# A second transfer of the edge features replaced by a copy on ScalarE

## The chip, the cores and the metric

The kernel runs on one core of one Trainium2 chip. The metric is the device time of one execution in microseconds; three executions of the kernel before took 4943.95, 4955.2 and 4957.94 us, median 4955.2.

## The reference, cut to what matters

A graph layer on 12,500 nodes with 64 features and 412,500 edges with 32 features each, sorted by destination. Everything is float32.

```
h    = relu(layernorm(x))
h0   = edge_attr @ W0 + b0                       # 32 -> 64, for every edge
g    = gelu(gelu(h0) @ W1 + b1) @ W2 + b2        # 64 -> 64 -> 64
score = (h0 + g) @ W3 + b3                       # 64 -> 64
msg  = h[src] * score
sums = segment_sum(msg, dst);  cnt = number of edges of each dst
out  = x + (sums / max(cnt, 1)) @ Wo + bo
```

## The kernel before, in words

The edges are cut into 403 blocks of 1024, each in two halves of 512. Since everything behind the second gelu is linear, the kernel multiplies W2, W0, b0, b2, b3 with W3 once, into a 97-row matrix `w_last`; its right-hand side is `act_in`, with 64 rows of the second gelu, 32 rows of the raw edge features and one row of ones. So the edge features of a block are needed twice: as `pair` (64 partitions, the two halves one above the other, 512 columns) for the first matmul, and as rows 64 to 95 of `act_in` (32 partitions, the two halves side by side) for the last. Both come from DRAM, in two transfers of 128 KB.

A block passes these steps, each named by its function or line:

- `gather` (L329), GpSimd: eight indirect transfers per block that fetch the normalised rows of `h` for 128 source nodes each, into a ring of 16 blocks. After the first 16 blocks, GpSimd waits before each block b+16 for the message of block b, and before every second one also for the score of block b+8 (`LAG`, L350). This is the only thing that stops it.
- `first` (L431), TensorE: `pair` times W0, to `ps_h0`. Bumps h0_done.
- ScalarE, first gelu (L386), to `g1`. Then the second gelu (L391), in two instructions, from `ps_h1` to `act_in`, once `second` is done.
- `second` (L437), TensorE: `g1` times W1, to `ps_h1`.
- `last` (L446), TensorE: eight tiles of `act_in`, 97 by 128, times `w_last`, to `ps_s`. It waits for the second transfer of the block (`attr_in`, L441) and for both gelus.
- `message` (L615), VectorE: score times gathered rows, to `msg`. It waits for `last` and for the gather.
- `sums` (L455), TensorE: `msg` of eight tiles times a one-hot matrix (L607) of the destinations within a window of 64, to `ps_w`; VectorE adds it to `acc` (L720).

TensorE's order in the steady state is written out by hand (`step`, L502): second(b), first(b+1), sums(b-1), last(b). ScalarE's is first gelu of b, second gelu of b, and so on. The names `ps_sa` and `ps_sb` in the profile are the buffers of even and odd blocks; the same holds for the other pairs.

The SP queue issues the loads. For each block b its loop `ahead` (L277) waits for h0_done of b, issues the `pair` load of block b+4, waits for the score of b, and issues the `act_in` load of block b+4; both buffers are rings of four (`IN_RING`). Once per eight blocks it waits for a message and loads gather indices.

Before the loop come the layernorm of all nodes (VectorE and ScalarE), with the raw rows of the first six blocks gathered meanwhile, and the window plan of the blocks; near the end, after block 390, the output of most nodes is made between two blocks.

Of the kernel before, what the change touches and what calls it, by code (L numbers as in the profile page):

```python
# [24 lines left out]
ACT = mybir.ActivationFunctionType  # L25
AX_X = mybir.AxisListType.X

P = 128
N = 12500
D = 64  # L30
DE = 32
E = 412500
TILES = 8
HALF = TILES // 2 * P
# [16 lines left out]
IDX_GROUPS = 4  # L51
LAG = 8
IN_RING = 4
RAW = 6
LN_ROWS = 25
SPLIT = 112
# [18 lines left out]
def edge_gated_layer(nc, x, edges, src, dst, dst_rows, weights, out):  # L75

    with ExitStack() as ctx:
        def sb(name, shape, dt=F32):
            return ctx.enter_context(nc.sbuf_tensor(name, shape, dt))
# [4 lines left out]
        def sem(name):  # L84
            return ctx.enter_context(nc.semaphore(name))
# [33 lines left out]

        idx = sb("idx", [P, IDX_GROUPS, IDX_GROUP, TILES], I32)  # L120
        pair = sb("pair", [2 * DE, IN_RING, HALF])
        act_in = sb("act_in", [D + DE + 1, IN_RING, 2, HALF])
        g1 = sb("g1", [P, 2, HALF])
        rows = sb("rows", [P, G_RING, TILES, D])

# [4 lines left out]
        fill = sb("fill", [P, 2])  # L130
# [33 lines left out]
        plan_ready = sem("plan_ready")  # L164

        pair_in = [sem(f"pair_in{s}") for s in range(IN_RING)]
        attr_in = [sem(f"attr_in{s}") for s in range(IN_RING)]
        idx_in = [sem(f"idx_in{q}") for q in range(IDX_GROUPS)]
        gathered = [sem(f"gathered{s}") for s in range(G_RING)]
        h0_done = sem("h0_done")  # L170
        g1_done = sem("g1_done")
        h1_done = sem("h1_done")
        g2_done = sem("g2_done")
        score_done = sem("score_done")
        gathers_begun = sem("gathers_begun")
        first_hot = sem("first_hot")
# [20 lines left out]

        jobs = [(LN_ROWS, NP)] * LN_STEPS + [(2 * TILES, P)] * (RAW // 2)
        ln_y = ln_d[0:EP, :, :, :].rearrange("p k n d -> p (k n) d")
# [16 lines left out]
        def uses(b, ring):  # L216

            return (b >> ring.bit_length() - 1) + 1
# [8 lines left out]
        def _(sp):  # L227
# [6 lines left out]
            def load_pair(b, s):  # L234
                sp.dma_start(pair[:, s % IN_RING, :],
                             edges[one(b), :, :, :].rearrange("o g f j -> (o g f) j")
                             ).then_inc(pair_in[s % IN_RING], 16)

            def load_attr(b, s):
                sp.dma_start(act_in[D:D + DE, s % IN_RING, :, :],  # L240
                             edges[one(b), :, :, :].rearrange("o g f j -> f (o g) j")
                             ).then_inc(attr_in[s % IN_RING], 16)

            load_idx(0, 0)
            for c in range(LN_STEPS):
                cols = slice(c * LN_ROWS, (c + 1) * LN_ROWS)
# [8 lines left out]
            sp.dma_start(wp[:, :], weights).then_inc(weights_in, 16)  # L255
            for b in range(2):
                load_pair(b, b)
                load_attr(b, b)
            load_idx(1, 1)
            sp.dma_start(dst_i[:, :, :], dst).then_inc(dst_in, 16)  # L260
            for b in range(2, IN_RING):
                load_pair(b, b)
                load_attr(b, b)
            for part in range(2, IDX_GROUPS):
                load_idx(part, part)
            sp.dma_start(x_late[:, :, :], x[N_EARLY:N, :].rearrange("(t p) d -> p t d", p=NP)
# [9 lines left out]

            def ahead(b, s):  # L277

                sp.wait_ge(h0_done, b + 1)
                load_pair(b + IN_RING, s + IN_RING)  # L280

                sp.wait_ge(score_done, b + 1)
                load_attr(b + IN_RING, s + IN_RING)

            GROUPS = -(-NB // IDX_GROUP)
            TURNS = GROUPS // IDX_GROUPS - 1
# [31 lines left out]
        def _(pool):  # L318
# [14 lines left out]

            for b in range(RAW):
                gather(b, b, x)
# [20 lines left out]
        @block.scalar  # L356
        def _(act):

            def ln_act(k, n, parts):
                act.wait_ge(ln_centred, k + 1)  # L360
                if k >= 2:

                    act.wait_ge(ln_var_ready, k - 1)
                act.activation(ln_sq[0:parts, k % 2, 0:n, :], ln_d[0:parts, k % 4, 0:n, :],
                               ACT.Square).then_inc(ln_squared, 1)

            def ln_root(k, n, parts):
                act.wait_ge(ln_var_ready, k + 1)
                act.activation(ln_std[0:parts, k % 4, 0:n], ln_var[0:parts, k % 4, 0:n],
                               ACT.Sqrt).then_inc(ln_std_ready, 1)  # L370

            def store_h(k):
                act.wait_ge(h_ready, k + 1)
                cols = slice(k * LN_ROWS, (k + 1) * LN_ROWS)
                for p0, p1 in ((0, SPLIT), (SPLIT, NP)):
                    act.dma_start(h_nodes[p0:p1, cols, :], ln_d[p0:p1, k % 4, :, :]).then_inc(h_out, 16)

            def clear_acc(k):
                n = (N + WIN) // LN_STEPS
                act.activation(acc[:, k * n:(k + 1) * n], fill[0:DC, 0:1].to_broadcast([DC, n]), ACT.Copy  # L380
                               ).then_inc(acc_zero, 1)

            def gelus(b, s):

                act.wait_ge(h0_done, b + 1)
                act.activation(g1[:, s % 2, :], ps_h0[s % 2][:, :], ACT.Gelu, bias=b0  # L386
                               ).then_inc(g1_done, 1)

                act.wait_ge(h1_done, b + 1)
                for g in range(2):  # L390
                    act.activation(act_in[0:D, s % IN_RING, g, :],  # L391
                                   ps_h1[s % 2][g * D:(g + 1) * D, :], ACT.Gelu,
                                   bias=wp[g * D:(g + 1) * D, C_B1:C_B1 + 1]
                                   ).then_inc(g2_done, 1)


            act.wait_ge(fill_ready, 1)
            act.activation(act_in[D + DE:D + DE + 1, :, :, :].rearrange("p s g j -> p (s g j)"),
                           fill[D + DE:D + DE + 1, 1:2].to_broadcast([1, IN_RING * 2 * HALF]),
                           ACT.Copy).then_inc(ones_ready, 1)  # L400
            for k in range(LN_STEPS + 1):
                if k < LN_STEPS:
                    ln_act(k, *jobs[k])
                if k >= 1:
                    ln_root(k - 1, *jobs[k - 1])
                if k >= 2:
                    store_h(k - 2)
                if k >= 1:
                    clear_acc(k - 1)
            store_h(LN_STEPS - 1)  # L410
            act.wait_ge(weights_in, 16)
            gelus(0, 0)
            for k in range(LN_STEPS, len(jobs) + 1):
                if k < len(jobs):
                    ln_act(k, *jobs[k])
                if k > LN_STEPS:
                    ln_root(k - 1, *jobs[k - 1])
            blocks_loop(act, 1, NB, IN_RING, gelus)


        @block.tensor
        def _(pe):
# [15 lines left out]
                          ).then_inc(h1_done, 1)  # L438

            def last(b, s):  # L440
                pe.wait_ge(attr_in[s % IN_RING], uses(b, IN_RING) * 16)  # L441

                pe.wait_ge(g2_done, (b + 1) * 2)
                for t in range(TILES):
                    g, j = t % 2, t // 2
                    mm = pe.matmul(ps_s[s % 2][:, t * D:(t + 1) * D],  # L446
                                   act_in[:, s % IN_RING, g, j * P:(j + 1) * P],
                                   w_last[:, :], start=(t == 0), stop=(t == TILES - 1),
                                   skip_group_check=True)
                mm.then_inc(score_done, 1)  # L450
# [340 lines left out]
def one(b):  # L791

    return bass.ds(b, 1)
# [52 lines left out]
```

## Time and profile before

| | |
|---|---|
| median of three runs | 4955.2 us (4943.95 to 4957.94) |
| profiled execution | 4910.35 us, its span 4908.4 us |
| granted TensorE clock | 0.999 of full speed |
| TensorE busy, matmuls | 3760.6 us, 77% of the span |
| TensorE busy, weight loads | 2533.1 us, 52% |
| GpSimd busy | 3082.5 us, 63% |
| ScalarE busy | 987.5 us, 20% |
| VectorE busy | 708.9 us, 14% |
| DMA engines | 46 GB/s; the software queue (gathers) 9.9%, the SP queue 8.4% |

All shares are over the whole span. A busy share says how full an engine is, not what it waits for; idle time of an engine costs only where the engine is the one that others wait for. In the rows below, a timeline row gives the start in us, the duration in us, the engine, the line, the operation, and in brackets how long the engine was idle before and what the profile names as releaser. "remote" as releaser means that the profile found no instruction of this core whose end fits the end of the wait.

### The profile page before, as it was taken

Reading aid. Unit: us, or ns where it says so; the run is one execution under the profiler, and the core shown is the slowest. Engines: PE = TensorE matmul, PEld = TensorE weight load, DVE = VectorE, ACT = ScalarE, POOL = GpSimd, SP = SyncE. Lnnn points to the kernel's source line nnn. Section 1 sums busy time; section 2 is a strip of 40 time slices with the busy share of each in tenths; the row PEclk is TensorE's granted clock in tenths of the full one; section 3 lists DMA queues with packets and bytes.
Section 4 is the critical chain, followed back from the end, with each engine's and each line's share of the span. In section 5 each row is a group of like instructions: output and inputs, shape, how many; then the busy total and the mean of one; then the engine's idle time right before and its main releaser. Section 6 shows DMA issues by size and latency. Waiting matters only on the chain.

```text
span 4908.4 us, 44284 instructions
## 1 busy us (share of the span) xinstructions
PE 3760.6 (77%) x14718; PEld 2533.1 (52%) x14719; DVE 708.9 (14%) x1349; ACT 987.5 (20%) x1332; POOL 3082.5 (63%) x3228
## 2 busy tenths in 40 slices
PE   2487777777777777777777777777777777777788
PEld 1355555555555555555555555555555555555566
DVE  5011111111111111111111111111111111111122
ACT  3112112221122211221122211222112121121211
POOL 7366666666666666666666666666666666666661
PEclk9999999999999999999999999999999999999999
DMA  4111111111111111111111111111111111111111
GB/s 122 28 46 44 45 44 46 46 45 44 44 46 46 44 45 44 46 47 44 44 45 45 46 44 44 44 45 47 44 44 46 44 47 44 44 46 44 46 37 47
DMA packets 223796, 227.46 MB, mean 46 GB/s; under 512 B 118540, under 2 KB 118669, under 8 KB 223352
## 3 DMA queue, kind: packets, MB, share of 16 engines
q0 software_dynamic: 103136, 105.82, 9.9%
q1 hardware_dynamic: 119968, 117.76, 8.4%
q10 hardware_dynamic: 616, 3.20, 0.2%
q14 instruction: 68, 0.56, 0.0%
q8 instruction: 8, 0.13, 0.0%
HBM read 220.11 MB, written 6.40 MB: 46 GB/s over the span
## 4 chain that ended last, share of the span: by engine, by line
another core or an unknown queue 63%; PE 25%; DVE 4%; DVEq 3%; issue 3%; POOL 1%; ACT 0%; DMA 0%; ACTq 0%; POOLq 0%
PE ps_sb L446 14%; PE ps_wa L455 8%; DVE msg L615 3%; DVEq L715 2%; POOL rows L329 1%; DVEq L614 1%; PE ps_sa L446 1%; PE ps_h1a L437 0%; PE ps_h0a L431 0%; PE ps_h0b L431 0%; PE ps_wb L455 0%; PE ps_h1a L484 0%; PE ps_h1b L437 0%; DVE acc L720 0%
## 5 line engine op out<-in xcount | busy, mean ns | idle before, releaser
L329 POOL DMA_INDIRECT rows<-h_rows,idx x3175 | 3026.5, 953 | 1739.0 <-issue 1005.5
L455 PE MATMUL ps_wa<-ln_sq,msg 128*65 128x64 f32 x3230 | 407.2, 319 | 1035.2 <-DVE msg L615 1035.2
L455 PEld LDWEIGHTS ps_wa<-ln_sq,msg 128*65 128x65 f32 x3230 | 369.7, 229 | 1348.6 <-DVE msg L615 1335.1
L391 ACT ACTIVATE act_in<-ps_h1b,wp 64x512 f32<-64x512 f32 x402 | 275.0, 684 | 2446.5 <-remote 2377.6
L446 PE MATMUL ps_sa<-w_last,act_in 97*128 97x64 f32 x3232 | 729.9, 420 | 11.1 <-ACT act_in L391 9.2
L446 PE MATMUL ps_sb<-w_last,act_in 97*128 97x64 f32 x3216 | 728.1, 421 | 0.6 <-ACT act_in L391 0.6
L446 PEld LDWEIGHTS ps_sa<-w_last,act_in 97*128 97x128 f32 x3232 | 711.9, 332 | 13.0 <-ACT act_in L391 9.0
L446 PEld LDWEIGHTS ps_sb<-w_last,act_in 97*128 97x128 f32 x3216 | 710.4, 333 | 2.3 <-issue 1.5
L615 DVE TENSOR_TENSOR msg<-ps_sa,rows 128x512 f32<-128x512 f32 x202 | 139.7, 691 | 3034.6 <-remote 2973.3
L391 ACT ACTIVATE act_in<-ps_h1a,wp 64x512 f32<-64x512 f32 x404 | 276.4, 684 | 1308.7 <-PE ps_h1a L437 1019.2
L455 PEld LDWEIGHTS ps_wb<-ln_sq,msg 128*65 128x65 f32 x3216 | 368.1, 229 | 303.5 <-issue 302.9
L437 PE MATMUL ps_h1b<-g,wp 128*128 128x512 f32 x402 | 406.4, 1112 | 35.7 <-ACT g L386 29.9
L431 PE MATMUL ps_h0a<-pair,wp 64*128 64x512 f32 x404 | 418.5, 1137 | 1.9 <-issue 1.9
L437 PE MATMUL ps_h1a<-g,wp 128*128 128x512 f32 x404 | 408.3, 1114 | 15.1 <-ACT g L386 13.4
L431 PE MATMUL ps_h0b<-pair,wp 64*128 64x512 f32 x402 | 416.5, 1138 | 0.0
L455 PE MATMUL ps_wb<-ln_sq,msg 128*65 128x64 f32 x3216 | 405.6, 319 | 1.5 <-issue 1.5
L615 DVE TENSOR_TENSOR msg<-ps_sb,rows 128x512 f32<-128x512 f32 x201 | 139.0, 692 | 985.9 <-PE ps_sb L446 905.8
L607 DVE TENSOR_TENSOR ln_sq<-dst_i,iota 128x512 f32<-128x512 f32 x403 | 277.8, 690 | 8.4 <-issue 8.4
L431 PEld LDWEIGHTS ps_h0a<-pair,wp 64*128 64x128 f32 x404 | 101.2, 309 | 304.3 <-issue 304.2
L431 PEld LDWEIGHTS ps_h0b<-pair,wp 64*128 64x128 f32 x402 | 100.3, 310 | 302.4 <-issue 302.4
L386 ACT ACTIVATE g<-ps_h0b,wp 128x512 f32<-128x512 f32 x201 | 138.2, 687 | 89.9 <-PE ps_h0b L431 51.5
L386 ACT ACTIVATE g<-ps_h0a,wp 128x512 f32<-128x512 f32 x202 | 138.9, 688 | 12.4 <-PE ps_h0a L431 5.5
(63 smaller groups left out, 719.4 us busy)
## 6 DMA issues: line engine op xcount, KB each, us to landing
pair<-in_edges SPq DMA_DIRECT2D x403, 128.0 KB
act_in<-in_edges SPq DMA_DIRECT2D x403, 128.0 KB
rows<-h_rows,idx POOLq DMA_INDIRECT x3175
xs<-in_x SPq DMA_DIRECT2D x4, 700.0 KB
h_rows<-ln_d ACTq DMA_DIRECT2D x4, 700.0 KB
dst_i<-in_dst SPq DMA_DIRECT2D x1, 1612.0 KB
idx<-in_src SPq DMA_DIRECT2D x50, 32.0 KB
rows<-in_dst_rows SPq DMA_DIRECT2D x4, 384.0 KB
```

The source lines that it names most:

```text
L329: pool.indirect_dma_start(rows[:, slot, t, :], None, table, bass.IndirectOffsetOnAxis(ap=idx[:, part, at, t:t + 1], axis=0),).then_inc(gat ...
L386: act.activation(g1[:, s % 2, :], ps_h0[s % 2][:, :], ACT.Gelu, bias=b0).then_inc(g1_done, 1)
L391: act.activation(act_in[0:D, s % IN_RING, g, :], ps_h1[s % 2][g * D:(g + 1) * D, :], ACT.Gelu, bias=wp[g * D:(g + 1) * D, C_B1:C_B1 + 1]). ...
L431: pe.matmul(ps_h0[s % 2][:, :], w0, pair[:, s % IN_RING, :], start=True, stop=True).then_inc(h0_done, 1)
L437: pe.matmul(ps_h1[s % 2][:, :], w1, g1[:, s % 2, :], start=True, stop=True).then_inc(h1_done, 1)
L446: mm = pe.matmul(ps_s[s % 2][:, t * D:(t + 1) * D], act_in[:, s % IN_RING, g, j * P:(j + 1) * P], w_last[:, :], start=(t == 0), stop=(t == ...
L455: last = pe.matmul(window, msg[:, s % 2, t, :], onehot[:, t, :], start=(t == 0), stop=(t == n - 1))
L607: return dve.tensor_tensor(to, rel.unsqueeze(2).to_broadcast([P, TILES, WIN]), iota_tiles, ALU.is_equal)
L614: dve.wait_ge(gathered[s % G_RING], (uses(b, G_RING) - 1) * 16 * TILES + 16 * n)
L615: dve.tensor_tensor(msg[:, s % 2, 0:n, 0:D], ps_s[s % 2][:, 0:n * D].rearrange("p (t d) -> p t d", d=D), rows[:, s % G_RING, 0:n, :], ALU. ...
L715: base = dve.value_load(base_b[0:1, one(b)], min_val=0, max_val=N - 1)
```

## The change

The second transfer is gone. In its place, ScalarE copies the two halves of `pair` (32 partitions by 512 each, two instructions) into rows 64 to 95 of `act_in`, after the first gelu of the block and before its wait for `second`. `act_in` becomes a ring of two blocks instead of four. The semaphores `attr_in` and `g2_done` go; one semaphore `act_in_done` is bumped by the two copies and the two gelus of the block. `last` waits for four bumps per block, in one wait instead of two. SP waits for the copies of block b (instead of h0_done of b) before it loads the `pair` of block b+4, and no longer waits for a score. Nothing protects the slot of `act_in` by a wait of its own: the copies of b come after h0_done of b, and TensorE issues first(b) after last(b-2). The row of ones is written over a ring of two.

```
+ACT_RING = 2
-        act_in = sb("act_in", [D + DE + 1, IN_RING, 2, HALF])
+        act_in = sb("act_in", [D + DE + 1, ACT_RING, 2, HALF])
...
-            def load_attr(b, s):
-                sp.dma_start(act_in[D:D + DE, s % IN_RING, :, :],
-                             edges[one(b), :, :, :].rearrange("o g f j -> f (o g) j")
-                             ).then_inc(attr_in[s % IN_RING], 16)
...
             def ahead(b, s):
-                sp.wait_ge(h0_done, b + 1)
+                sp.wait_ge(act_in_done, b * 4 + 2)
                 load_pair(b + IN_RING, s + IN_RING)
-                sp.wait_ge(score_done, b + 1)
-                load_attr(b + IN_RING, s + IN_RING)
...
                 act.activation(g1[:, s % 2, :], ps_h0[s % 2][:, :], ACT.Gelu, bias=b0
                                ).then_inc(g1_done, 1)
+                for g in range(2):
+                    act.activation(act_in[D:D + DE, s % ACT_RING, g, :],
+                                   pair[g * DE:(g + 1) * DE, s % IN_RING, :], ACT.Copy
+                                   ).then_inc(act_in_done, 1)
                 act.wait_ge(h1_done, b + 1)
                 for g in range(2):
-                    act.activation(act_in[0:D, s % IN_RING, g, :],
+                    act.activation(act_in[0:D, s % ACT_RING, g, :],
                                    ps_h1[s % 2][g * D:(g + 1) * D, :], ACT.Gelu,
                                    bias=wp[g * D:(g + 1) * D, C_B1:C_B1 + 1]
-                                   ).then_inc(g2_done, 1)
+                                   ).then_inc(act_in_done, 1)
...
             def last(b, s):
-                pe.wait_ge(attr_in[s % IN_RING], uses(b, IN_RING) * 16)
-                pe.wait_ge(g2_done, (b + 1) * 2)
+                pe.wait_ge(act_in_done, (b + 1) * 4)
```

## Rows read from the trace of the kernel before

**Rows 1.** The page's busy time, share of the span and instructions of each engine.

```profile
PE 3760.6 (77%) x14718; PEld 2533.1 (52%) x14719; DVE 708.9 (14%) x1349; ACT 987.5 (20%) x1332; POOL 3082.5 (63%) x3228
```

**Rows 2.** Groups of instructions, GpSimd: busy us, mean ns | idle before, releasers.

```profile
L329 POOL DMA_INDIRECT rows<-h_rows,idx x3175 | 3026.5, 953 | 1739.0 <-issue 1005.5 <-remote 670.7 <-PE ps_sa L446 62.8
L329 POOL DMA_INDIRECT rows<-in_x,idx x48 | 55.6, 1159 | 17.4 <-issue 14.3 <-DMA idx<-in_src 3.0
```

**Rows 3.** Waits of GpSimd: us in total, times, longest us.

```profile
POOL rows L329 <- issue: 1019.9, 3043, 41.9
POOL rows L329 <- remote: 670.7, 178, 4.1
POOL rows L329 <- PE ps_sa L446: 62.8, 1, 62.8
```

**Rows 4.** Timeline of all engines, one turn of two blocks in mid-run.

```profile
3613.03 1.39 ACT L391 ACTIVATE act_in<-ps_h1b,wp 64x512 f32<-64x512 f32 x2 [12.67 <-remote]
...
3613.73 0.94 POOL L329 DMA_INDIRECT rows<-h_rows,idx  x1 [3.82 <-remote]
...
3614.45 0.69 ACT L386 ACTIVATE g<-ps_h0a,wp 128x512 f32<-128x512 f32 x1
...
3621.61 1.40 ACT L391 ACTIVATE act_in<-ps_h1a,wp 64x512 f32<-64x512 f32 x2 [6.48 <-issue]
3622.29 0.69 SPq L235 DMA_DIRECT2D pair<-in_edges  x1
...
3624.90 3.62 PE L446 MATMUL ps_sa<-w_last,act_in 97*128 97x64 f32 x16
...
3630.26 2.07 PE L431 MATMUL ps_h0a<-pair,wp 64*128 64x512 f32 x2
...
3632.54 0.94 POOL L329 DMA_INDIRECT rows<-h_rows,idx  x1 [0.31 <-issue]
3636.54 0.33 SPq L240 DMA_DIRECT2D act_in<-in_edges  x1
...
3636.72 0.69 DVE L615 TENSOR_TENSOR msg<-ps_sa,rows 128x512 f32<-128x512 f32 x1 [15.31 <-remote]
...
3637.47 0.95 POOL L329 DMA_INDIRECT rows<-h_rows,idx  x1 [3.98 <-remote]
```

**Rows 5.** Timeline of VectorE while GpSimd stands still (178 to 241 us).

```profile
187.54 0.69 DVE L615 TENSOR_TENSOR msg<-ps_sa,rows 128x512 f32<-128x512 f32 x1 [82.23 <-remote]
...
204.00 0.69 DVE L615 TENSOR_TENSOR msg<-ps_sa,rows 128x512 f32<-128x512 f32 x1 [7.43 <-PE ps_sa L446]
...
213.18 0.69 DVE L615 TENSOR_TENSOR msg<-ps_sb,rows 128x512 f32<-128x512 f32 x1 [7.42 <-PE ps_sb L446]
```

**Rows 6.** Groups of instructions, ScalarE, the whole span.

```profile
L391 ACT ACTIVATE act_in<-ps_h1a,wp 64x512 f32<-64x512 f32 x404 | 276.4, 684 | 1308.7 <-PE ps_h1a L437 1019.2 <-issue 249.8 <-remote 34.6
...
L386 ACT ACT_TABLE_LOAD x101 | 129.6, 1283 | 1.8
L380 ACT ACTIVATE acc<-fill 65x3141 f32<-65x3141 f32 x4 | 11.3, 2817 | 2.1 <-issue 2.1
...
L398 ACT ACTIVATE act_in<-fill 1x4096 f32<-1x4096 f32 x1 | 3.6, 3612 | 0.0
L364 ACT ACTIVATE ln_sq<-ln_d 128x1024 f32<-128x1024 f32 x3 | 3.2, 1058 | 25.6 <-issue 20.6 <-DVE ln_d L582 5.0
```

**Rows 7.** Timeline of ScalarE in a stretch without gathers.

```profile
199.17 0.69 ACT L386 ACTIVATE g<-ps_h0b,wp 128x512 f32<-128x512 f32 x1
205.64 0.68 ACT L391 ACTIVATE act_in<-ps_h1b,wp 64x512 f32<-64x512 f32 x1 [5.79 <-PE ps_h1b L437]
```

**Rows 8.** The page's DMA issues (KB each), and GpSimd's line L329 (ns min/median/max).

```profile
act_in<-in_edges SPq DMA_DIRECT2D x403, 128.0 KB
...
L329 POOL DMA_INDIRECT rows<-h_rows,idx x3175: 942/947/3490, 74.3 to 4838.5; - x199
```

**Rows 9.** The page's costliest groups: the matmuls of `last`.

```profile
L446 PE MATMUL ps_sa<-w_last,act_in 97*128 97x64 f32 x3232 | 729.9, 420 | 11.1 <-ACT act_in L391 9.2
```

More of the change, by code:

```diff
@@ L166, in edge_gated_layer @@
         pair_in = [sem(f"pair_in{s}") for s in range(IN_RING)]
-        attr_in = [sem(f"attr_in{s}") for s in range(IN_RING)]
         idx_in = [sem(f"idx_in{q}") for q in range(IDX_GROUPS)]
@@ L172, in edge_gated_layer @@
         h1_done = sem("h1_done")
-        g2_done = sem("g2_done")
+        act_in_done = sem("act_in_done")
         score_done = sem("score_done")
@@ L257, in _ @@
                 load_pair(b, b)
-                load_attr(b, b)
             load_idx(1, 1)
@@ L262, in _ @@
                 load_pair(b, b)
-                load_attr(b, b)
             for part in range(2, IDX_GROUPS):
@@ L387, in gelus @@
                                ).then_inc(g1_done, 1)
+                for g in range(2):
+                    act.activation(act_in[D:D + DE, s % ACT_RING, g, :],
+                                   pair[g * DE:(g + 1) * DE, s % IN_RING, :], ACT.Copy
+                                   ).then_inc(act_in_done, 1)
                 act.wait_ge(h1_done, b + 1)
                 for g in range(2):
-                    act.activation(act_in[0:D, s % IN_RING, g, :],
+                    act.activation(act_in[0:D, s % ACT_RING, g, :],
                                    ps_h1[s % 2][g * D:(g + 1) * D, :], ACT.Gelu,
                                    bias=wp[g * D:(g + 1) * D, C_B1:C_B1 + 1]
-                                   ).then_inc(g2_done, 1)
+                                   ).then_inc(act_in_done, 1)
             act.wait_ge(fill_ready, 1)
             act.activation(act_in[D + DE:D + DE + 1, :, :, :].rearrange("p s g j -> p (s g j)"),
-                           fill[D + DE:D + DE + 1, 1:2].to_broadcast([1, IN_RING * 2 * HALF]),
+                           fill[D + DE:D + DE + 1, 1:2].to_broadcast([1, ACT_RING * 2 * HALF]),
                            ACT.Copy).then_inc(ones_ready, 1)
@@ L446, in last @@
                     mm = pe.matmul(ps_s[s % 2][:, t * D:(t + 1) * D],
-                                   act_in[:, s % IN_RING, g, j * P:(j + 1) * P],
+                                   act_in[:, s % ACT_RING, g, j * P:(j + 1) * P],
                                    w_last[:, :], start=(t == 0), stop=(t == TILES - 1),
```

## The prediction, made before the changed kernel was run

> **What bounds the kernel now.** I read the busy shares first [rows 1]. TensorE leads with 77%, GpSimd follows with 63%, ScalarE has 20%. The shares don't say who waits for whom, so I went to the groups of instructions of GpSimd [rows 2] and to its waits [rows 3]. The reader is to see that GpSimd alone accounts for almost the whole span. Its first 48 gathers take 55.6 + 17.4 = 73.0 us with their gaps, its other 3175 take 3026.5 + 1739.0 = 4765.5 us; with 1.0 us before them that is 4839.5, the end of the last gather, and a tail of 68.9 us behind it makes the span of 4908.4. The profiled execution took 4910.35 us, 0.9% less than the median of the runs shown (4955.2); I work in the profile's time and carry the result over in proportion.
>
> Within the 1739.0 us of gaps: a gather always has 0.30 us before the next, so 3175 x 0.30 = 952 us is the cost of issuing, and a gather costs 0.95 + 0.30 = 1.25 us. One pause of 62.8 us stands at the start. The 178 pauses named "remote" are 3.77 us each (670.7 / 178), 3.47 more than the usual gap: 617 us. The rest is 107 us of odd longer gaps [rows 3].
>
> The timeline shows what a pause is [rows 4]. GpSimd starts at 3613.73, issues 16 gathers for two blocks until 3633.48, and restarts at 3637.47: a turn of 23.7 us for two blocks, 19.8 of it gathers. In the pause it waits for a score. But TensorE's records have the score (`ps_sa`) begin at 3624.90 and take 3.62, so it is done at 3628.5, and the last matmul of the pass (`ps_h0a`) at 3632.3. Yet VectorE, which needs only that score, starts at 3636.72 (idle for 15.31), ScalarE, which needs `ps_h1b`, and SP, which needs the score, resume at the same moment (3636.54 to 3636.6). So for about 8 us nobody learns that the score is done, and all learn it together, 3.1 us after the last gather has ended. While GpSimd stands still, the same chain is prompt: messages follow each other at 9.18 us (204.00, 213.18), TensorE back to back [rows 5]. And the one at 187.54 had VectorE idle for 82.23 us, through the stream of gathers of the start. I read this as: in a long stream of gathers, TensorE's completions reach the others late, and they are let go when the stream ends. Why, the rows don't say. What follows is that a turn is 16 gathers plus the pause, and that the pause ends in a fixed order: stream ends, signals come, GpSimd sees the score. TensorE has 2 x 9.18 = 18.4 us of work in 23.6 and is not the limit; it is in some 20 blocks at the start and the end.
>
> **The change part by part.** *The copies.* 806 of them, 32 partitions by 512. The nearest rows are the Copy instructions of 4096 and 3141 elements, 3612 and 2817 ns: 0.832 ns per element and 204 ns on top, so 630 ns for 512. The other end is the gelu of the same length, 684 ns [rows 6]. I take 630, as the same function, from SBUF: 1.26 us per block, 508 us of ScalarE in all (1.37 at the high end, 551); its share goes from 20 to 30%. By the Trainium skill (ScalarE: Activation LUTs, What ACT_TABLE_LOAD costs) an ACTIVATE without a pointer operand takes 186 ns and 0.833 ns per element, which would give 613; that changes no step.
>
> Where do they lie? In the turn, after the first gelu, 3614.45 + 0.69 = 3615.1, to 3616.4; the next instruction is the second gelu at 3621.61, which waits for TensorE. 5.2 us of cover are left. In the other half the first gelu ends at about 3625.2, and the next is at 3636.6. In the stretch where TensorE is the limit: first gelu ends at 199.9, second at 205.64, a window of 5.8 us for 1.26 [rows 7]. The first gelu itself, which TensorE needs soonest, stands before the copies. Path: 0 in all of them. If the cover were gone, all 1.26 x 403 = 508 us would be on it; nothing in the rows takes 4.5 us away, so I keep 0 to 25 us (1.26 x 20 blocks bound by TensorE) as the range of this term.
>
> *Table loads.* ScalarE loads a table once per four blocks (101 loads of 1283 ns). That Copy could need another table than Gelu isn't shown by a row directly: Copy followed Sqrt (L380) without a load of its own, and Square (L364) ran on both sides of a Gelu without one [rows 6]. At worst there are two loads per block, 2.57 us, beside 1.26 us of copies: 3.8 in windows of 5.8 and more, so they would be hidden too. I take 0; the high end is hidden as well. The Trainium skill (ScalarE: Activation LUTs, Table sets: the hidden batching unit) says that copy is in every set, so there would be no added load; no row here has a Copy between two Gelus.
>
> *The removed transfer.* 403 transfers of 128 KB, 53 of 227 MB [rows 8], with a wait and an issue of SP each. `last` waits for a transfer issued four blocks earlier, some 47 us at the turn's pace; it never ends that wait last (what ended the waits of L446 were the gelus, 9.2 us in all [rows 9]). So 0 from the wait. Can the gathers gain? Their mean is 953 ns and their median 947 [rows 8]; if all of the 6 ns were collisions with other transfers, half of which go, the gain lies between 0 and 6 x 3175 = 19 us. I take 0 to 10. Below nothing: less traffic can't slow a gather.
>
> *The moved load.* `pair` of block b+4 is now issued after the copies, 2 to 3 us later than h0_done of b, in the turn at about 3616.5 and 3626.5 instead of 3613.6 and 3622.3. SP has nothing else queued but that and the index load once per eight blocks, whose wait for a message is unchanged and which holds up the next `pair` by a few us at most; the data is needed by first(b+4), over 35 us later. 0. What I can't price from a row is whether a load issued in the middle of the stream changes when TensorE's signals begin to be late (below).
>
> *The single wait of `last`* instead of two: TensorE's records are back to back either way, 0. *The ring of two*: the copies of b are behind h0_done of b, which is behind last(b-2) in TensorE's order, so no wait is added. *The row of ones* is half as long (1.7 us less) at the start, beside the first loads: 0.
>
> **The sum**, in the profile's time: 4908.4 + 0 (copies) + 0 (tables) - 0 to 10 (traffic) + 0 (load) = 4898 to 4908, say 4904. Per turn, the 16 gathers and the pause are not touched. Carried over (x 1.009): 4950 us, against 4955.2. The likeliest case's own range is 4935 to 4970.
>
> **The rivals.** *A, the pause gets shorter (faster).* TensorE's signals and SP's issues may share a path that the gathers crowd; with half of the issues and with the 16 signals of each removed transfer gone, the pause may shrink. For it: the delay is about signals, and SP takes 0.69 us to issue a load in the stream, 0.33 in the pause [rows 4]. Against it: the release follows the end of the gathers, when SP has long been idle. 0.3 us less on 178 pauses is 53 us: 4900. If the lateness went altogether, GpSimd would not pause: 617 us less, 4908 - 617 = 4291, carried over 4332. The first 0.20, the second 0.04.
>
> *B, the lateness begins sooner (slower).* One mechanism: in the first half of the turn the odd block's score is still seen at once; SP's `pair` load is now issued at +3.4 us of the turn, between the release and that score. If a transfer issued within the stream is what sets off the lateness (in rows 4 the second `pair` load, 3622.29, is just before it), the score of the odd block would be held to the end of the stream too, and TensorE's second pass of 9.18 us would come after it. Price: 9.18 us per turn in which it happens; in one of ten, 18 x 9.18 = 165 us, 5120; in all, 178 x 9.18 = 1634, 6600. It decides early: two such turns are 18 us, over the bound below. Against it: the same loads were issued at the turn's beginning and the signals after them were prompt. 0.10.
>
> *C, the copies are not covered.* As above, 25 us where TensorE is the limit, 4980; 0.08.
>
> **How the numbers follow.** Forecast 0.58; A 0.24; B 0.10; C 0.08. What this kernel's measurement can tell from no change is about 0.3%, 15 us. Faster: A in full, 0.24, and 0.05 of the forecast, where the traffic gives its full 19 us; 0.29. Slower: B and C, 0.18, less the small ones: 0.17. Within: 0.54. For the range I leave out the second case of A (0.04), B (0.10) and a little of the rest: 4885 to 4995.
>
> **What would show it right or wrong.** Right: 16 gathers and a pause of about 3.8 us per turn, 178 or so pauses, L329's sum of busy and gaps within 20 us of 4765; copies at about 630 ns, ending over 4 us before the second gelu starts; still about 101 table loads at L386. A: pauses shorter than 3.5 us, or fewer of them. B: VectorE's wait before the message of the odd block (`ps_sb`) grows past 5 us, and turns of over 30 us appear. C: blocks at 9.18 us become longer. The forecast is wrong if the time moves by over 15 us; the step to fail would be that nothing but the gathers and the end of their stream sets the turn.

## The result and the profile after

The changed kernel takes 4997.6 us (median of 6 runs, 4976.91 to 5071.86) where the kernel before, in the same runs, takes 4955.07 (4943.95 to 4959.7). The ratio is 1.0093, with a 95% interval of 1.0066 to 1.0121: slower by 0.9%. The forecast was no change, 4950 us. One of the six runs of the changed kernel, the one of 5071.86 us, is 1.9% above the fastest and is left out of the ratio. The profiled execution took 5014.18 us with a span of 5012.3, at a granted TensorE clock of 0.511. Its span is 103.9 us above that of the profiled execution of before, though the medians differ by only 42.5, so the two traces show more than the change. The experiments below met five chips, on which the kernel before took between 4195.2 and 4963.88 us. For that reason a second trace of the changed kernel is read beside this one, e5_after_again. It comes from a chip on which before takes 4904.85 us, close to the 4910.35 of the profile of before. No run gave traces of both kernels on one chip that pauses, so a difference between two traces is weaker evidence than a ratio.

The page's busy line of the changed kernel, to be read beside [rows 1]:

```profile
PE 3773.9 (75%) x14718; PEld 2539.4 (51%) x14719; DVE 708.9 (14%) x1349; ACT 1490.0 (30%) x2138; POOL 3093.1 (62%) x3228
```

ScalarE went from 20 to 30% by 806 instructions; the other engines do what they did. The groups of GpSimd beside [rows 2], and its waits beside [rows 3]:

```profile
L319 POOL DMA_INDIRECT rows<-h_rows,idx x3175 | 3037.2, 957 | 1828.7 <-issue 1032.5 <-remote 676.7 <-PE ps_sa L440 119.5
```

```profile
POOL rows L319 <- issue: 1046.8, 3043, 61.7
POOL rows L319 <- remote: 676.7, 168, 4.4
POOL rows L319 <- PE ps_sa L440: 119.5, 11, 63.3
```

The gathers cost 10.7 us more (3037.2 against 3026.5), their gaps 89.7 us more (1828.7 against 1739.0). So the time is in the pauses. About 20 us of it is one wait, the longest of the kind "issue" (61.7 against 41.9). The 168 pauses named "remote" are now 4.03 us each (3.77 before), and ten of the eleven named "PE ps_sa" are new: a little over 5.6 us each, (119.5 - 63.3) / 10.

One turn of two blocks and the start of the next, to be read beside [rows 4] (start, duration, engine, line, operation, idle before and releaser):

```profile
3608.56 0.94 POOL L319 DMA_INDIRECT rows<-h_rows,idx  x1 [4.40 <-remote]
...
3609.86 1.28 ACT L380 ACTIVATE act_in<-pair 32x512 f32<-32x512 f32 x2
...
3610.42 3.62 PE L440 MATMUL ps_sb<-w_last,act_in 97*128 97x64 f32 x16
...
3615.87 0.69 DVE L609 TENSOR_TENSOR msg<-ps_sb,rows 128x512 f32<-128x512 f32 x1 [6.25 <-remote]
3615.90 1.39 ACT L386 ACTIVATE act_in<-ps_h1a,wp 64x512 f32<-64x512 f32 x2 [4.76 <-issue]
...
3618.61 1.28 ACT L380 ACTIVATE act_in<-pair 32x512 f32<-32x512 f32 x2
...
3619.61 3.62 PE L440 MATMUL ps_sa<-w_last,act_in 97*128 97x64 f32 x16
...
3627.28 0.94 POOL L319 DMA_INDIRECT rows<-h_rows,idx  x1 [0.30 <-issue]
3631.65 1.39 ACT L386 ACTIVATE act_in<-ps_h1b,wp 64x512 f32<-64x512 f32 x2 [11.75 <-remote]
3631.79 0.69 DVE L609 TENSOR_TENSOR msg<-ps_sa,rows 128x512 f32<-128x512 f32 x1 [13.75 <-remote]
3632.35 0.94 POOL L319 DMA_INDIRECT rows<-h_rows,idx  x1 [4.13 <-remote]
...
3634.35 3.62 PE L440 MATMUL ps_sb<-w_last,act_in 97*128 97x64 f32 x16
...
3638.36 0.69 DVE L609 TENSOR_TENSOR msg<-ps_sb,rows 128x512 f32<-128x512 f32 x1 [4.81 <-PE ps_sb L440]
```

The stream of 16 gathers lasts from 3608.56 to 3628.22, 19.7 us as before. The even block's score is done at 3623.23 by TensorE's records, and VectorE's message on it starts at 3631.79, 8.6 us later and 3.57 us after the stream's end (3.24 in the turn of [rows 4]: 3636.72 - 3633.48). GpSimd goes on 0.56 us later. The two pairs of copies end at 3611.1 and 3619.9, and neither has anything waiting behind it: ScalarE's second gelus start 4.8 and 11.8 us later. The odd block's message shows something new. At 3615.87 it comes 1.83 us after the end of its score (3610.42 + 3.62) and is named "remote"; a turn later, at 3638.36, it comes 0.4 us after it (3634.35 + 3.62 = 3637.97), as before.

The same over the whole span, VectorE's messages, first of the kernel before, then of the changed one (busy, mean ns, idle before and releasers):

```profile
L615 DVE TENSOR_TENSOR msg<-ps_sa,rows 128x512 f32<-128x512 f32 x202 | 139.7, 691 | 3034.6 <-remote 2973.3 <-PE ps_sa L446 61.2
L615 DVE TENSOR_TENSOR msg<-ps_sb,rows 128x512 f32<-128x512 f32 x201 | 139.0, 692 | 985.9 <-PE ps_sb L446 905.8 <-remote 56.8 <-issue 23.2
```

```profile
L609 DVE TENSOR_TENSOR msg<-ps_sa,rows 128x512 f32<-128x512 f32 x202 | 139.7, 692 | 2876.5 <-remote 2735.0 <-PE ps_sa L440 141.5
L609 DVE TENSOR_TENSOR msg<-ps_sb,rows 128x512 f32<-128x512 f32 x201 | 139.0, 692 | 1255.7 <-remote 743.6 <-PE ps_sb L440 512.1
```

The wait before the odd block's message grew by 269.8 us (the one before the even block's fell by 158.1), and 743.6 us of it (56.8 before) no longer end with a matmul that the profile can name. This can't be put down to the change, though. The kernel of e10 below has both transfers, no copies, and the same time as before on its chip (1.0004), and its trace shows the same two marks, the late odd message and many pauses named "PE ps_sa":

```profile
L614 DVE TENSOR_TENSOR msg<-ps_sb,rows 128x512 f32<-128x512 f32 x201 | 139.0, 692 | 1328.0 <-remote 726.0 <-PE ps_sb L445 601.9
...
POOL rows L329 <- PE ps_sa L445: 157.5, 21, 64.3
```

In e5_after_again, which lost 0.95%, the "remote" share is 183.5 us only. ScalarE's groups, beside [rows 6]:

```profile
L380 ACT ACTIVATE act_in<-pair 32x512 f32<-32x512 f32 x806 | 505.4, 627 | 19.6
L386 ACT ACTIVATE act_in<-ps_h1a,wp 64x512 f32<-64x512 f32 x404 | 275.9, 683 | 1184.4 <-issue 746.4 <-PE ps_h1a L432 247.1 <-remote 185.9
...
L376 ACT ACT_TABLE_LOAD x101 | 129.6, 1283 | 1.8
```

The copies take 627 ns each, and there are still 101 table loads of 1283 ns.

GpSimd's waits in e5_after_again, whose span is 4961.1 us:

```profile
POOL rows L319 <- issue: 1022.2, 3043, 43.9
POOL rows L319 <- remote: 679.1, 171, 4.3
POOL rows L319 <- PE ps_sa L440: 101.3, 8, 64.2
```

Against [rows 3] the sum is 49.2 us larger, with 3.97 us for a "remote" pause and seven more pauses that end with `ps_sa`. These take 3.75 to 8.95 us and only two of them are over 5 us; six lie in the first turns after the standstill, up to 419 us. I set the start of each block's first gather against that of before, in the two traces: e5_after_again is 0.9 us behind at block 15, 2.3 at block 16 (the restart after the first standstill), 12.4 at block 26, 46.4 at block 375 and 51.8 at block 402. So some 12 us are lost by the end of the first five turns after the standstill, 34 in the steady state (0.2 us per turn of two blocks) and 5 around the output stage. The profile after has the same shape: 0.3 at block 16, 17.2 at 26, 77.1 at 375, 100.3 at 402.

### The profile page after: what moved, and what is told of

Read it like the earlier page. It is cut to its first block, busy times and chain, and to the rows that moved or that the text cites. A ratio compares the mean times of both kernels' runs of the same rounds, so it can differ in the third digit from the quotient of the medians.

```text
span 5012.3 us, 44449 instructions
## 1 busy us (share of the span) xinstructions
PE 3773.9 (75%) x14718; PEld 2539.4 (51%) x14719; DVE 708.9 (14%) x1349; ACT 1490.0 (30%) x2138; POOL 3093.1 (62%) x3228
## 4 chain that ended last, share of the span: by engine, by line
another core or an unknown queue 71%; PE 16%; DVEq 4%; issue 3%; DVE 3%; POOL 1%; ACT 1%; DMA 0%; ACTq 0%; POOLq 0%
PE ps_sb L440 8%; PE ps_wa L449 4%; DVEq L709 3%; DVE msg L609 2%; PE ps_sa L440 1%; POOL rows L319 1%; DVEq L608 1%; PE ps_h1b L432 1%; PE ps_h0a L426 1%; DVE acc L714 0%; PE ps_h1a L478 0%; PE ps_h1b L478 0%; DVE ln_sq L601 0%; PE ps_wb L449 0%
## 5 line engine op out<-in xcount | busy, mean ns | idle before, releaser
L319 POOL DMA_INDIRECT rows<-h_rows,idx x3175 | 3037.2, 957 | 1828.7 <-issue 1032.5
L380 ACT ACTIVATE act_in<-pair 32x512 f32<-32x512 f32 x806 | 505.4, 627 | 19.6
L609 DVE TENSOR_TENSOR msg<-ps_sb,rows 128x512 f32<-128x512 f32 x201 | 139.0, 692 | 1255.7 <-remote 743.6
```

What stands on the lines that cost most here:

```text
L319: pool.indirect_dma_start(rows[:, slot, t, :], None, table, bass.IndirectOffsetOnAxis(ap=idx[:, part, at, t:t + 1], axis=0),).then_inc(gat ...
L380: act.activation(act_in[D:D + DE, s % ACT_RING, g, :], pair[g * DE:(g + 1) * DE, s % IN_RING, :], ACT.Copy).then_inc(act_in_done, 1)
L609: dve.tensor_tensor(msg[:, s % 2, 0:n, 0:D], ps_s[s % 2][:, 0:n * D].rearrange("p (t d) -> p t d", d=D), rows[:, s % G_RING, 0:n, :], ALU. ...
```

## The experiments

Each was timed in 5 rounds against the kernel before on the same chip; ratios have their 95% interval. "Pauses" are those of GpSimd. Line numbers in rows are those of each kernel.

**The parts alone**, on a chip where before takes 4908.79 us. e1_copies_added: the kernel before with two copies more per block, from the weights into a spare buffer, and everything else as it was.

```
+                for g in range(2):
+                    act.activation(spare[...], wp[g * DE:(g + 1) * DE, 0:HALF], ACT.Copy
+                                   ).then_inc(g2_done, 1)
-                pe.wait_ge(g2_done, (b + 1) * 2)
+                pe.wait_ge(g2_done, (b + 1) * 4)
```

> The kernel before, both transfers kept, and two ScalarE copies per block added behind the first gelu, from the weights into a spare buffer (their result is not used), bumping the semaphore that the last matmul waits for. A turn of two blocks took 23.58 us before and takes 23.91 after; of the 0.33, 0.25 lies between the end of the gather stream and the message. Theory S (ScalarE's added instructions and bumps make TensorE's signals later): turn 23.9, time about 0.9% over before, 4995. Theory T (the removed transfer is the cause): turn 23.6, 4955. Theory L (the pair load issued 3 us later is the cause): 23.6, 4955.

Measured 1.0013 (1.0004 to 1.0021). The copies are not quite free, but 6 us of 4909 are far from the loss.

e2_transfer_out: the kernel before without the second transfer and its waits, and without copies; the feature rows of `act_in` are filled with zeros once at the start, so the features are left out of the last matmul. (By block 15 this trace is 0.6 us behind the one of before, so the filling costs next to nothing.)

```
-                sp.wait_ge(score_done, b + 1)
-                load_attr(b + IN_RING, s + IN_RING)
...
-                pe.wait_ge(attr_in[s % IN_RING], uses(b, IN_RING) * 16)
```

> The kernel before without the second transfer, its waits on TensorE and on SP, and without any copy: the edge rows of the score operand are zero, so that term is left out of the result. Pair load as before at h0_done. Theory T: turn 23.9, 4995. Theory S and theory L: turn 23.6 or less, 4955 or less.

Measured 1.0040 (1.0026 to 1.0054). To take a transfer away, with its waits, and put nothing in its place costs 20 us. The group of its gathers shows where, beside [rows 2]:

```profile
L324 POOL DMA_INDIRECT rows<-h_rows,idx x3175 | 3017.3, 950 | 1769.7 <-issue 1008.4 <-remote 687.6 <-PE ps_sa L441 73.6
```

The gathers are 9.2 us shorter, their gaps 30.7 us longer (28.1 longer than those of e1 on the same chip, 1741.6). One pause of 9.5 us at 4763 us is 5.7 of these 30.7.

e3_transfer_kept: the changed kernel with the second transfer back, into a spare buffer, with SP's wait for the score and TensorE's wait for it.

```
+                sp.wait_ge(score_done, b + 1)
+                load_attr(b + IN_RING, s + IN_RING)      # into spare
...
+                pe.wait_ge(attr_in[s % IN_RING], uses(b, IN_RING) * 16)
```

> The changed kernel, and the second transfer issued again at its old place (SP waits for the score, TensorE waits for it), into a spare buffer that nobody reads. Theory T: back to turn 23.6, 4955. Theory S: 23.9, 4995, as after. Theory L: 23.9, 4995.

Measured 1.0035 (1.0021 to 1.0048): the copies, the ring and the later `pair` load alone cost 17 us. The groups of e1 and of e3, from one chip, tell that what e3 has over e1 is not in the pauses:

```profile
L330 POOL DMA_INDIRECT rows<-h_rows,idx x3175 | 3023.5, 952 | 1741.6 <-issue 1006.0 <-remote 673.8 <-PE ps_sa L452 61.8
...
L332 POOL DMA_INDIRECT rows<-h_rows,idx x3175 | 3034.8, 956 | 1742.3 <-issue 1006.2 <-remote 671.4 <-PE ps_sa L454 64.7
```

The gaps are equal, and the gathers take 11.3 us more.

e4_early_load: the changed kernel with SP waiting for h0_done, as before. For that the copies read the weights, not `pair`; the features are left out.

```
-                sp.wait_ge(act_in_done, b * 4 + 2)
+                sp.wait_ge(h0_done, b + 1)
...
-                                   pair[g * DE:(g + 1) * DE, s % IN_RING, :], ACT.Copy
+                                   wp[g * DE:(g + 1) * DE, 0:HALF], ACT.Copy
```

> The changed kernel, but the copies read the weights instead of the pair, so that SP may load the pair at h0_done as before (the edge term of the score is wrong). Theory L: back to turn 23.6, 4955. Theory S and theory T: 23.9, 4995.

Measured 1.0043 (1.0029 to 1.0057), within the error of e2. So transfer out, copies in and early load cost 21 us together, with the ring of two and the single wait in it.

**Repeat, ring and moment**, on a chip where before takes 4904.85 us. e5_after_again is the changed kernel as it is.

> The changed kernel itself, unaltered, on the chip of this batch, since the first batch ran on a chip where the kernel before takes 4908.8 us, not 4955. If the loss belongs to the change and not to the chip: 0.9% over before. If the parts found so far just add (copies 0.13%, transfer out 0.40%): 0.5%.

Measured 1.0095 (1.0079 to 1.0110): the loss is there again. e6_late_load: e1 with the later moment of the `pair` load, `sp.wait_ge(g2_done, b * 4 + 2)` in place of `sp.wait_ge(h0_done, b + 1)`.

> The first experiment (both transfers kept, copies added into a spare buffer; 0.13% over before) with one more edit: SP waits for the two copies of the block before it loads the pair of four blocks on, as in the changed kernel. The changed kernel with the second transfer kept was 0.35% over before. Theory L (the later load costs): 0.35%. Rival (the smaller ring of act_in or the single wait costs): 0.13%.

Measured 1.0032 (1.0020 to 1.0043). The later moment costs 0.2% over e1 even where the second transfer stays, as in e3. Its gathers take 3038.3 us, and its "remote" pauses 670.7, just as before. e7_ring_of_four: the changed kernel with `ACT_RING = 4`.

> The changed kernel with ACT_RING = 4. If the ring of two is a part of the loss, this is faster than the changed kernel of the same batch by 0.1% or more; otherwise the same.

Measured 1.0102 (1.0085 to 1.0118), as e5: the ring of two has no part. x1_wait_each_block is the kernel before, with GpSimd waiting for the score of b+8 before every block.

```
-                if s % 2 == 0:
-                    pool.wait_ge(score_done, b + (G_RING - LAG + 1))
+                pool.wait_ge(score_done, b + (G_RING - LAG + 1))
```

> The kernel before, but GpSimd waits for a score before every block, not every second one. If TensorE's signals only become late after some 5 to 9 us of gathers in a row, streams of 8 gathers (9.9 us) with shorter pauses: per block 10.0 + about 1.5, 11.5 against 11.8 now, 2% faster. Rival (each pause costs its 3.8 us whatever the stream): 13.8 per block where the wait isn't met, up to 17% slower; or, if the wait for odd blocks is always met already, no change.

Measured 0.9976 (0.9967 to 0.9985), 11 us faster than before. It is the only version that beat both kernels.

**Waits and what keeps SP busy**, on a chip where before takes 4963.88 us. e8_dummy_wait gives TensorE back a second wait ahead of `last`, on something long met: `pe.wait_ge(pair_in[s % IN_RING], uses(b, IN_RING) * 16)`, added to the changed kernel.

> The changed kernel with a second wait put back on TensorE in front of the last matmul, on pair_in of the block, which is always met. No transfer comes back. In all kernels so far the second transfer and the wait for it on TensorE came and went together. Theory W (the wait on TensorE's sequencer is what matters, since it keeps it from running ahead): 0.35% over before, like the changed kernel with the transfer kept. Theory T (the transfer itself or SP's issue of it matters): 0.95%, like the changed kernel.

Measured 1.0143 (1.0126 to 1.0161), from three runs that lie between 5012.96 and 5038.39 us. The second wait brings nothing back, and this is more than the change lost elsewhere; the change itself was not run on this chip, so how much of it is the wait's stays open. e10_wait_moved takes it away from TensorE in the kernel before: the wait on `attr_in` stands on ScalarE ahead of the second gelu, not on TensorE.

```
+                act.wait_ge(attr_in[s % IN_RING], uses(b, IN_RING) * 16)
...
-                pe.wait_ge(attr_in[s % IN_RING], uses(b, IN_RING) * 16)
```

> The kernel before with both transfers and no copies; only the wait for the second transfer is moved from TensorE's last matmul to ScalarE, ahead of its second gelu. Theory W: 0.3 to 0.4% over before, as in the kernel without the transfer. Theory T: same as before, within 0.1%.

Measured 1.0004 (0.9994 to 1.0015): no change. So no part of the loss that these two runs can show is due to the merged wait of `last`. e11_load_at_score: the changed kernel, with SP waiting for the score of b before it loads `pair` of b+4, as it once did for the second transfer: `sp.wait_ge(score_done, b + 1)`.

> The changed kernel, but SP loads the pair of four blocks on when the block's score is done, so at the two moments of the turn at which the second transfer was issued before, and not in the middle of the gather stream. Theory L (the time of the load within the stream): 0.35 to 0.45% over before, as with the early load. Rival (the loss comes from the number of waits or transfers alone): 0.95%.

Measured 1.0099 (1.0082 to 1.0116), what the change lost on its two chips, and below e8 on this one. Since the change itself was not run here, this shows that the loss is there without a load after the copies, but not that the moment of the load has no part in it.

e9_transfer_no_wait: the changed kernel with the second transfer into a spare buffer, TensorE not waiting for it, and SP waiting for the landing of the one four blocks before.

```
+                sp.wait_ge(score_done, b + 1)
+                sp.wait_ge(attr_in[s % IN_RING], uses(b, IN_RING) * 16)
+                load_attr(b + IN_RING, s + IN_RING)      # into spare
```

> The changed kernel with the second transfer issued again at its old place into a spare buffer, but no wait for it on TensorE (SP waits for the landing of the one four blocks before instead). Theory T: 0.35% over before. Theory W: 0.95%.

Measured 1.1076 (1.1044 to 1.1108). No expectation of mine had a loss of this size. Its named pauses are 6.22 us each, (1062.0 - 64.7 + 110.3) / 178, and its timeline (weight loads and other rows left out) shows the order of events of rival B of the prediction:

```profile
3209.25 0.69 DVE L625 TENSOR_TENSOR msg<-ps_sa,rows 128x512 f32<-128x512 f32 x1 [6.82 <-PE ps_sa L456]
3209.82 0.95 POOL L335 DMA_INDIRECT rows<-h_rows,idx  x1 [5.32 <-PE ps_sa L456]
...
3214.60 3.62 PE L456 MATMUL ps_sb<-w_last,act_in 97*128 97x64 f32 x16
...
3228.58 0.94 POOL L335 DMA_INDIRECT rows<-h_rows,idx  x1 [0.30 <-issue]
...
3230.08 0.69 DVE L625 TENSOR_TENSOR msg<-ps_sb,rows 128x512 f32<-128x512 f32 x1 [19.08 <-remote]
...
3237.66 2.02 PE L448 MATMUL ps_h1b<-g,wp 128*128 128x512 f32 x2
...
3238.08 0.69 DVE L625 TENSOR_TENSOR msg<-ps_sa,rows 128x512 f32<-128x512 f32 x1 [6.25 <-PE ps_sa L456]
3238.66 0.94 POOL L335 DMA_INDIRECT rows<-h_rows,idx  x1 [9.13 <-PE ps_sa L456]
```

The odd block's score is done at 3218.2, 8.4 us into the stream, but its message starts at 3230.08, after the stream's end at 3229.52, with VectorE idle for 19.08 us. Then TensorE's next pass has to be made, and GpSimd's pause is 9.13 us. The turn is 28.8 us long instead of 23.7, so 5.1 longer, where rival B had said 9.18. In the turn of the profile after, the odd block's score begins 1.9 us into the stream (3610.42 against 3608.56). Here it begins 4.8 us in, since TensorE still had `second` and `first` of the pass before to do when the stream began (until 3212.85). That the later score is what makes the difference is argued from such turns, not shown by an experiment.

**Chips without pauses.** These four ask how both kernels' traces differ on one chip, and which part the moment of the load has beside the copies. e12_before_again is the kernel before. e13_load_after_next_first is the changed kernel with `sp.wait_ge(h0_done, b + 3)` in place of the wait for the copies; that is the first matmul of b+2, so a load starts at a moment like that of before, with less lead. e14_after_again is the changed kernel, and x2_after_wait_each_block the changed kernel with the edit of x1.

> The kernel before itself, for a trace on the same chip as the three below. Ratio 0.999 to 1.001; its mean turn in mid-run about 0.2 us (1%) shorter than that of the changed kernel on this chip, with stream and pause to be told apart.

> The changed kernel with its true copies from pair, but SP waits for h0_done of b+2 (the first matmul of two blocks later) before it loads pair of b+4, instead of the copies of b: a load is issued at the moments of the kernel before, two blocks less ahead. Theory M (the later moment of the one load in the turn costs half of the loss, as the pair early load against load at score suggests): ratio 1.003 to 1.006. Rival D (copies that read pair, or the removed transfer itself, make the loss, wherever the load lies): 1.008 to 1.011. If data comes late, as it is only two blocks ahead: over 1.02.

> The changed kernel on the chip of these runs: 1.008 to 1.011. Its added time lies in the pauses between streams of 16 gathers, most of it in blocks 16 to 60 and after block 380.

> The changed kernel, with GpSimd waiting for the score of b+8 before every block instead of every second (the edit that gave 0.9976 on the kernel before). If the loss comes from scores that are held past a stream of 16 gathers, shorter streams take part of it away: 1.004 to 1.008. If the loss has nothing to do with the length of the streams: the same 0.24% off, 1.006 to 1.009. Both overlap; below 1.004 would say that the rule of two blocks makes most of the loss, above 1.010 that it has no part.

On this chip the kernel before takes 4195.2 us, and the four give 1.0000 (0.9991 to 1.0009), 0.9999 (0.9990 to 1.0008), 1.0001 (0.9992 to 1.0010) and 0.9998 (0.9989 to 1.0007). The page, GpSimd's waits and VectorE's messages of e12_before_again, the same program as that of [rows 1 to 3]:

```profile
PE 3722.5 (89%) x14718; PEld 2500.6 (60%) x14719; DVE 709.2 (17%) x1349; ACT 986.3 (24%) x1332; POOL 3164.5 (75%) x3228
```

```profile
POOL rows L329 <- issue: 981.9, 3222, 0.3
POOL rows L329 <- DMA idx<-in_src: 3.0, 1, 3.0
```

```profile
L615 DVE TENSOR_TENSOR msg<-ps_sa,rows 128x512 f32<-128x512 f32 x202 | 139.7, 692 | 1656.2 <-DMA rows<-h_rows,idx 1598.7 <-PE ps_sa L446 57.5
L615 DVE TENSOR_TENSOR msg<-ps_sb,rows 128x512 f32<-128x512 f32 x201 | 139.1, 692 | 1670.4 <-DMA rows<-h_rows,idx 1616.4 <-PE ps_sb L446 53.9
```

No gap of GpSimd is longer than 3.0 us, and all but one are 0.3. The messages wait for the gathered rows, not for "remote". Here TensorE's completions are not held back while gathers are issued (`ps_h1b` ends at 3609.24, between gathers that never pause, and the second gelu starts at 3609.28), so a turn is 16 gathers and nothing else, 20.47 us from one odd block's message to the next (timeline of VectorE):

```profile
3601.25 0.69 DVE L615 TENSOR_TENSOR msg<-ps_sb,rows 128x512 f32<-128x512 f32 x1 [8.58 <-DMA rows<-h_rows,idx]
...
3621.72 0.69 DVE L615 TENSOR_TENSOR msg<-ps_sb,rows 128x512 f32<-128x512 f32 x1 [8.55 <-DMA rows<-h_rows,idx]
```

The changed kernel, e14_after_again, has the same waits, the one of 3.0 us too:

```profile
POOL rows L319 <- issue: 981.9, 3222, 0.3
```

The kernels of e13 and x2 were also run on another chip, as e15 and x3. It has no pauses either (before: 4201.49 us).

> The kernel of e13 (changed kernel, true copies, load issued at h0_done of b+2) again. Where GpSimd never pauses (the chip of e12 to e14, 4195 us): 1.000 again. Where it pauses after each stream (before at 4900 to 4965 us): theory M, 1.003 to 1.006; rival D, 1.008 to 1.011.

> The kernel of x2 (changed kernel, GpSimd waits for the score before every block) again. Without pauses: 1.000. With pauses: 1.004 to 1.008 if shorter streams take part of the loss away, 1.006 to 1.009 if they only give their own 0.24%; above 1.010 they have no part in it.

Measured 0.9999 (0.9990 to 1.0008) and 1.0000 (0.9991 to 1.0009). Whether the moment of the load or the copies from `pair` make the second half of the loss stays open.

## Why the prediction was wrong

*The copies* were sized and placed rightly: 627 ns against 630 forecast, 505 us of ScalarE, and over 4.7 us of cover in both halves of the turn. Alone they cost 6 us (e1), against 0 to 25. *The table loads* stayed at 101 where a Copy now stands between two Gelus. That is what the Trainium skill (ScalarE: Activation LUTs, Table sets: the hidden batching unit) states, that copy is in every set. The estimate from the Trainium skill (ScalarE: Activation LUTs, What ACT_TABLE_LOAD costs), 613 ns for a copy, is 14 below the measured 627. *The ring of two* (e7) cost nothing, as said, and neither did *the single wait*, as far as e8 and e10 can tell. Rival C falls: where TensorE is the limit, messages follow each other at 9.18 us after as before (4985.68 and 4994.86 in the profile after, [rows 5] before).

*The removed transfer* was put at 0 to 10 us of gain, with "Below nothing: less traffic can't slow a gather". The reason was sound for the gathers themselves (3017.3 us in e2 against 3026.5), but it looked only at them. The loss of 20 us in e2 is in the gaps (1769.7 against 1739.0). So the gain in the gathers came as forecast, 9.2 us, but the term as a whole had the wrong sign, because the bound left the pause out.

*The moved load* was put at 0, with an open question about the moment. It costs about 0.2% where the second transfer stays (e6 over e1: 1.0032 against 1.0013, on two chips; e3: 1.0035). By one trace each this part is in the gathers (3023.5 us in e1, 3034.8 in e3, 3038.3 in e6), which the prediction had looked at for traffic only.

*The step that failed* is the one named in the prediction: "that nothing but the gathers and the end of their stream sets the turn". A turn is still 16 gathers and a pause that begins with the end of the stream, but the pause is no constant. It went from 3.77 to 3.97 us (e5) and 4.03 us (the profile after) for the ordinary ones, and a few turns get a second pass of TensorE behind the stream. The chip doesn't explain e5: on the same chip e6, which keeps the second transfer, has 3.77 us (670.7 / 178). The sum of the gathers and their gaps, forecast within 20 us of 4765, came out at 4816.7 in e5 (3028.5 + 1788.2) and 4865.9 in the profile after. I had taken the row for a pause as a fixed cost because the rows of one kernel show one value of it. Nothing in them said that it would stay so when SP's issues and ScalarE's instructions move, and the range gave this 0.10, by rival B alone.

*Rival B* has its sign right and its mechanism at most in part. Of its signs, the wait before the odd block's message grew past 5 us (6.25 on average in the profile after, 5.38 in e5, 4.90 before), but it is 6.61 in e10 too, where nothing was lost; so the late odd score alone is no mark of the loss. Its price of 9.18 us per turn is reached nowhere: the turn of e9 shown is 5.1 us longer. In e5 the seven pauses ending with `ps_sa` that [rows 3] lack make 101.3 - 64.2 = 37.1 us (the longest is the standstill at the start); but they stand in place of ordinary ones of 3.97 us, so they explain 9 us of the 52. Most of the rest is 0.2 us in every ordinary pause, 34 us. That a `pair` load in the stream sets it off is not borne out: with the load at the score (e11) the loss is still 0.99%, on a chip where the change was not measured. *Rival A* had the sign wrong; with fewer issues the pauses got longer.

What the runs show, then: the loss was measured only where TensorE's completions are held back during a stream (1.0093 and 1.0095 for the change, 1.0099 to 1.0143 for e7, e8 and e11, which keep the loss; 1.0001 where there are no pauses), and it is made of at least two parts that don't add up simply. The transfer's removal gives 0.40% (e2), the copies 0.13% (e1), both together with an early load 0.43% (e4), and with the later load and true copies 0.95% (e5), where the parts would sum to some 0.7%. Taking the transfer away costs 0.3% where the load is early (1.0043 in e4 against 1.0013 in e1) and 0.6% where it is late (1.0095 in e5 against 1.0032 in e6, on one chip); copying from `pair` costs nothing more where the transfer stays (1.0035 in e3, 1.0032 in e6). What is open: why SP's second transfer keeps the pauses short, and whether its issue, its waits or its 16 completions per block do it. e9, which issues it but waits otherwise, is by far the slowest, so the transfer as such is not what helps. The wait on TensorE alone doesn't help either (e8); only e3, with the transfer and its two old waits, was near 0.35%, and that on another chip.

## What to carry to other kernels

A pause whose releaser the profile can't name was not a constant here: give it a range of its own on both sides, even when an edit only removes work beside it. When an engine's completion, by its records, lies many microseconds ahead of everyone who waits for it, look for the stream of instructions that ends just before they all resume, and count what the edit does within that stream. And take both kernels' traces on one chip before reading a difference of 1%: here the chip decides over 15%, over whether there is an effect at all, and over marks in a trace that look like a loss (e10).

## What the runs showed of the hardware that was not expected

**The same program has two regimes.** On three of the chips of the experiments it takes 4905 to 4964 us, with a pause of about 3.8 us after every 16 gathers; on two it takes 4195 and 4201 us without any pause. The gathers themselves are no faster there (979 ns on average, against 953). What puts a chip into one or the other isn't shown by any run.

**The granted clock of the profile doesn't tell the pace of the matmuls.** VectorE's first messages without waits for gathers, in e12_before_again at a granted clock of 1.00 in this stretch, and in x3_after_wait_each_block_b, also at 1.00:

```profile
99.47 0.69 DVE L615 TENSOR_TENSOR msg<-ps_sa,rows 128x512 f32<-128x512 f32 x1 [4.09 <-PE ps_sa L446]
...
104.29 0.69 DVE L615 TENSOR_TENSOR msg<-ps_sb,rows 128x512 f32<-128x512 f32 x1 [3.03 <-PE ps_sb L446]
...
109.14 0.69 DVE L615 TENSOR_TENSOR msg<-ps_sa,rows 128x512 f32<-128x512 f32 x1 [3.08 <-PE ps_sa L446]
```

```profile
104.00 0.69 DVE L607 TENSOR_TENSOR msg<-ps_sa,rows 128x512 f32<-128x512 f32 x1 [8.11 <-PE ps_sa L438]
...
113.16 0.69 DVE L607 TENSOR_TENSOR msg<-ps_sb,rows 128x512 f32<-128x512 f32 x1 [7.37 <-PE ps_sb L438]
...
122.35 0.69 DVE L607 TENSOR_TENSOR msg<-ps_sa,rows 128x512 f32<-128x512 f32 x1 [7.42 <-PE ps_sa L438]
```

A pass of TensorE takes 4.8 us in one and 9.2 us in the other. The windows of both kernels (TensorE, weight load, VectorE, ScalarE and GpSimd busy, granted clock, DMA share, GB/s) show what follows:

```profile
105.00:120.00 15.00, 15.00 (x110) 10.20 (x110) 4.89 (x11) 7.88 (x11) 11.40 (x12) 1.00 0.30 84
120.00:178.00 58.00, 53.29 (x323) 37.25 (x322) 12.72 (x25) 20.60 (x29) 43.99 (x47) 0.78 0.26 66
178.00:240.00 62.00, 56.19 (x218) 37.04 (x216) 9.20 (x18) 14.88 (x20) 47.37 (x49) 0.50 0.21 52
```

```profile
105.00:120.00 15.00, 15.00 (x62) 9.97 (x62) 2.32 (x5) 7.90 (x11) 11.34 (x13) 1.00 0.14 34
...
178.00:240.00 62.00, 62.00 (x247) 41.49 (x245) 10.06 (x21) 25.72 (x37) 47.47 (x48) 1.00 0.17 39
```

In e12 the clock is granted in full (2.4 GHz) while TensorE is busy without a break (15.00 of 15.00 us), then falls to 0.50 (1.2 GHz), and it is 0.50 from 1000 to 2000 us and from 4000 to 4100 us too. The 16 matmuls of `last` take 1.95 us at 106.97 us and 3.62 us at 1003.05 and 4004.87; in x3, at a granted 1.00, they take 3.62 us at 100.16, 201.13 and 4002.26. In the kernels that pause they take 3.62 us at a granted 0.50 (the turn of the profile after) as at 1.00 [rows 4]. So here a clock of 1.00 in the page stands for either pace, and the length of a known matmul tells which.
